# A token-mixing and LoRA feed-forward kernel: GpSimd's order of work ahead of the second pair of tiles

## The reference

```python
W = weights[condition]                                   # one 64x64 matrix of 16 for each batch
y = einsum('bct,bcd->bdt', x, W)
result = einsum('bnd,od->bno', y, W_base) + b_base
probs = softmax(einsum('bnd,ed->bne', y, W_gate))
top_p, top_i = top_k(probs, 2)                           # normalised to sum 1 -> route_w
h = einsum('bnd,erd->bner', y, A)
delta = einsum('bner,eor->bno', h * route_w[..., None], B)
out = x + result + delta * SCALING                       # SCALING = 1
```

## Time and profile before

| what | value |
|---|---|
| median of 3 runs | 952.94 us (952.38 to 955.5) |
| the profiled execution | 952.68 us, of which the span is 950.9 us |
| PE matmul busy | 938.5 us, 99% of the span |
| DVE, ACT, POOL busy | 430.8, 383.6, 543.9 us |
| chain that ended last | PE 93%, POOL 2%, each other engine or queue 1% or less |

### The profile page before, as it was taken

One profiled execution on the slowest core, in us unless ns is written; L12 is line 12 of the kernel. 1 busy time (PEld: TensorE's weight loads), 2 busy tenths in 40 slices (PEclk: granted clock), 3 DMA queues, 4 the chain that ended last, 5 costly groups with the idle time before them and its releaser, 6 DMA issues.

```text
span 950.9 us, 16849 instructions
## 1 busy us (share of the span) xinstructions
PE 938.5 (99%) x5462; PEld 881.5 (93%) x5462; DVE 430.8 (45%) x1333; ACT 383.6 (40%) x815; POOL 543.9 (57%) x514
## 2 busy tenths in 40 slices
PE   8899999999999999999999999999999999999998
PEld 6789999999999999999999999999999999999997
DVE  5774444434444434444444444344444344443444
ACT  6644434333344334343333343343433433433332
POOL 2956466545565554665555755556655557555560
PEclk9999999999999999999999999999999999999999
DMA  9333322233322333223333223332223332233312
GB/s 315 119 100 134 119 98 86 105 121 132 110 85 97 109 128 126 95 87 101 121 132 110 95 92 109 122 132 88 91 96 121 132 110 98 90 110 121 132 46 87
DMA packets 41452, 107.13 MB, mean 113 GB/s; under 512 B 4449, under 2 KB 8674, under 8 KB 41442
## 3 DMA queue, kind: packets, MB, share of 16 engines
q1 hardware_dynamic: 41440, 107.01, 32.7%
q10 hardware_dynamic: 2, 0.00, 0.0%
HBM read 73.43 MB, written 33.55 MB: 113 GB/s over the span
## 4 chain that ended last, share of the span: by engine, by line
PE 93%; POOL 2%; DMA 1%; issue 1%; SPq 1%; ACT 1%; DVE 1%; POOLq 0%; DVEq 0%
PE ps L791 55%; PE ps_r L791 18%; PE ps_out L809 10%; PE ps_out L819 9%; DMA w_sum<-in_w_t 1%; PE ps_hwt L815 1%; POOL s_lo L312 1%; POOL a_lo L308 0%; POOL s_sum L333 0%; ACT w_hi L416 0%; POOL s_sum L319 0%; SPq L220 0%; POOL s_sum L325 0%; SPq L224 0%; SPq L230 0%
## 5 line engine op out<-in xcount | busy, mean ns | idle before, releaser
L308 POOL TENSOR_TENSOR a_lo<-raw,a_hi 128x512 fp32r<-128x512 f32 x128 | 164.7, 1307 | 239.5 <-ACT a_hi L400 239.5
L610 DVE TENSOR_TENSOR z_sum<-ps,z_sum 128x448 f32<-128x448 f32 x155 | 96.8, 625 | 242.1 <-PE ps L791 242.0
L791 PE MATMUL ps<-w_hi,s_hi 128*128 128x448 f32 x496 | 183.7, 370 | 0.4 <-DVE z_sum L610 0.4
L791 PE MATMUL ps<-w_lo,s_hi 128*128 128x448 f32 x496 | 181.2, 365 | 0.0
L791 PE MATMUL ps<-w_hi,s_lo 128*128 128x448 f32 x496 | 179.7, 362 | 0.0
L791 PE MATMUL ps<-w_hi,a_hi 128*128 128x448 f32 x372 | 138.9, 373 | 3.4 <-POOL a_lo L308 3.4
L791 PE MATMUL ps_r<-r_lo,a_hi 128*128 128x264 f32 x496 | 140.8, 284 | 0.0
L791 PE MATMUL ps_r<-r_hi,a_hi 128*128 128x264 f32 x496 | 140.7, 284 | 0.0
L791 PE MATMUL ps_r<-r_hi,a_lo 128*128 128x264 f32 x496 | 140.6, 283 | 0.0
L791 PE MATMUL ps<-w_lo,a_hi 128*128 128x448 f32 x372 | 135.7, 365 | 0.0
L791 PE MATMUL ps<-w_hi,a_lo 128*128 128x448 f32 x372 | 135.6, 364 | 0.0
(11 more groups left out here) (97 smaller groups left out, 1592.9 us busy)
## 6 DMA issues: line engine op xcount, KB each, us to landing
raw<-in_x_t SPq DMA_DIRECT2D x128, 256.0 KB, 2.9
o_sb<-in_x SPq DMA_DIRECT2D x64, 512.0 KB, 3.9
out_x<-o_sb SPq DMA_DIRECT2D x62, 512.0 KB, 2.6
w_sum<-in_w_t SPq DMA_DIRECT2D x8, 448.0 KB, 9.3
r_raw<-in_w_t SPq DMA_DIRECT2D x4, 264.0 KB, 4.3
table_raw<-in_cond_w SPq DMA_DIRECT2D x2, 256.0 KB, 9.1
b_raw<-in_b_t SPq DMA_DIRECT2D x1, 512.0 KB, 11.0
out_x<-o_sb SPq DMA_DIRECT2D x2, 224.0 KB, 2.1
```

What stands on the lines that cost most here:

```text
L308: pool.tensor_tensor(a_lo[j][:], raw[j][:], as_f32(a_hi[j][:]), ALU.subtract).then_inc(s_a_lo[j], 1)
L610: return dve.tensor_tensor(to, bank[:, 0:NS], other, ALU.add)
L791: mm = pe.matmul(bank[:, 0:w.shape[-1]], a[:, k, :], w[:, k, :], start=(opens and k == 0 and q == 0), stop=(closes and k == KH - 1 and q = ...
```

## The change

POOL's order ahead of the second pair is written anew. The three sums S3, S1 and S2 stay first. Then the rests of A11 and A12 and the sum S4 come ahead of the rests of S3 and S1. No instruction is added or taken away, and nothing else in the program is touched.

```diff
             sum_s3(1, True)
             sum_s1(1, True)
             sum_s2(1, True)
-            s_rest(1, 3, s3[:], s3_hi, s3_lo)
-            s_rest(1, 1, s1[:], s1_hi, s1_lo)
             a_rest(1, A11)
             a_rest(1, A12)
             sum_s4(1)
+            s_rest(1, 3, s3[:], s3_hi, s3_lo)
+            s_rest(1, 1, s1[:], s1_hi, s1_lo)
             s_rest(1, 2, s2[:], s2_hi, s2_lo)
```

## The result

| | before | changed |
|---|---|---|
| median of 20 runs | 953.0 us (951.36 to 955.5) | 955.57 us (954.16 to 956.59) |
| the profiled execution | 952.68 us, span 950.9 | 955.73 us, span 954.0 |

The ratio is 1.0024, 95% interval 1.0018 to 1.0031: 0.24% slower, clear of noise but inside the 0.3% that the prediction counts as no change. The medians are 2.6 us apart, against 1.8 forecast; the prediction's limit for no change was 955.8, so 0.2 us were left.

The account below looks back on a forecast made before the run. PE, fully busy in the 29.00 us loop, was taken as the bound. P7 1.9 us later, less 0.1 at the LoRA wait, added 1.8 to the profiled 952.68: 954.5 us, range 951.0 to 956.8.

Parts of the forecast that it names:

- What bounds the kernel: In the loop PE is busy 29.00 of 29.00 us, so time won or lost before it stays so.
- What the change gives to PE: Second pair's start: P1 follows without idle at about 37.05, P2 starts at 40.50 instead of 45.66, 5.16 us earlier.
- What the earlier PE sets off: DVE's T rests shift 5.15 us onto POOL's A21, A22 and mix0 copies; taking turns, they delay PE's mixing to 54.73.
- The tie: DVE's rest of T3 against POOL's second copy into mix0: DVE starts 0.07 us before and goes first.
- The second case: Rival: the second copy into mix0 beats DVE's rest of T3; 951.2 to 952.8, centre 952.4 us; chance 0.28.
- The sum: From mixing at 54.73, 5.83 us of matmuls plus 1.67 for the clock: P7 at 62.2, 1.9 us later.
- The clock's fall: Behind PE's long idle ahead of the mixing, the lower clock costs 1.67 us, between 0 and 3.3.
- The wait at the LoRA rest: PE's later wait of 0.51 us for the LoRA rest at 69.90 may shrink; 0.1 us taken.
- No hindrance: Rival: POOL and DVE don't hinder each other, mix0 ready at 49.26, P7 5.2 us earlier; 947.5 us; chance 0.13.
- The slower case: Rival: DVE first, clock low twice as long behind PE's idle, another 1.67 us; 956.2 us; chance 0.14.

Follow-up runs that it names:

- experiment 2: Changed kernel with DVE's rest of T3 made to wait until both copies into mix0 are done: 952.69 us, ratio 0.9999.
- t1_holds: Changed kernel with DVE's rest of T1, and so that of T3, made to wait until mix0 is fetched: 951.08 us, ratio 0.9977.
- experiment 6: Changed kernel with POOL's rest of A12 and sum S4 moved behind the rests of S3 and S1: 950.4 us, ratio 0.9969.
- experiment 1: Changed kernel with the second pair's two copies into mix0 made ahead of the rest of S2: 949.85 us, ratio 0.9962.
- Experiment 8: Changed kernel with SP's load into A11 for the third pair held until the rest of S3 is made: 954.45 us, ratio 1.0023.
- filler: Changed kernel with 28 matmuls on zeros put in PE's gap ahead of the late mixing: 954.24 us, ratio 1.0011.
- filler_more: Changed kernel with 33 matmuls on zeros put in PE's gap ahead of the late mixing: 953.42 us, ratio 1.0008.
- 7: Kernel before, in its old order, with the two copies into mix0 made ahead of the rest of S2: 953.11 us, ratio 1.0002.
- 9: Changed kernel with early copies into mix0 and POOL's rests of A21 and A22 held until DVE's rest of T3: 955.09 us, ratio 1.0028.

## Why the prediction was right

**What bounds the kernel.** Right: the loop kept its full 29.00 us, and what PE lost ahead of it came out at the end, but for 0.4 us. ACT's copy of P1 comes 3.56 us later than before at the first loop pair (80.28 and 76.72) and 3.18 us at the last (921.10 and 917.92); no row shows where these 0.38 us went.

**What the change gives to PE.** Right. P1 starts without idle, P2 at 41.03 (40.50 and the 0.5 of the slow start), the last R matmul at 47.86 (47.22 and 0.64).

**What the earlier PE sets off.** Right in each step: T2's rest 2.72 us, A21 and A22 4.31, T1's rest 2.21, both copies above 2 us. Experiments 2 and 3 undo the meetings one by one by holding DVE, and the copies become short; experiment 6 does it by a later A12; 1 moves the copies out. Experiment 8 shows the same gap without the earlier load. That the earlier P2 is what moves DVE onto POOL is shown by 6 together with the profile.

**The tie.** Right, and steadier than its 0.07 us promised: DVE's T3 was first in the four profiled executions that leave the tie open (the changed kernel, `filler`, `filler_more`, `sp_later`), its second copy taking 2.11 us in each. The second case, at 0.28, was given too much; its time was right when experiment 2 forced it.

**The sum.** The gap is 7.25 us where 7.2 follow from the forecast's times. The clock's fall was mis-sized for this execution. From the mixing to P7 PE took 64.00 - 55.38 = 8.62 us, 2.79 above the 5.83 at full clock; the forecast took 1.67. The profiles in which PE waits for nothing else between the two give this, in us:

| kernel | gap ahead of the mixing | from the mixing to P7 | above 5.83 |
|---|---|---|---|
| changed | 7.25 | 8.62 | 2.79 |
| `sp_later` | 7.24 | 7.34 | 1.51 |
| `t3_holds` | 5.43 | 7.65 | 1.82 |
| `t1_holds` | 3.66 | 7.47 | 1.64 |
| `a12_later` | 2.18 | 5.94 | 0.11 |
| `filler` | 1.21 | 5.90 | 0.07 |

So 1.67 is near what three of the four long gaps cost, and the changed kernel's own profiled execution is the one far above it. A single price was wrong, and the two ends, 0 and 3.3, held all of them. P7's 3.69 us are about the forecast's 1.9, plus 0.65 for the later resumption (0.5 of it the slow start), plus 1.12 for the clock. The wait at the LoRA rest shrank by 0.08 us, from 0.51 to 0.43; 0.1 was taken. That the final number is as near as it is, 2.6 against 1.8, is in part luck: without the slow start P7 is 3.2 us late where 1.9 was forecast, and part of the difference is the 0.38 us of the loop, which nothing in the forecast foresaw.

**The rivals.** No hindrance (0.13) is refuted by the profile; its sign was right for what follows when the copies are out of the way (experiment 1). The slower case (0.14) named the clock as what could add to the forecast. It did, by two thirds of what that case gave, and its sign, a low stretch longer than 5 us, is there in this execution (0.50 over 5.9 us). In `sp_later`'s it is not: the clock is back at 1.00 from 58.50 us on, 3.1 us behind the gap.

## What to carry to other kernels

An engine that is late can shield its neighbours from each other. Before moving work ahead, shift everything that hangs on it by the gain, and look at what it lands on, here DVE instructions with two SBUF operands on POOL's. Then move the small thing that the critical engine waits for next, such as the 0.6 us of copies into `mix0`, ahead of the collision: the reorder alone lost 2.6 us, and with the copies moved it won 3.3. And before holding an engine back, see which load or buffer hangs on the end of its queue.

## What the runs showed of the hardware

The price of a PE gap in clock is not set by its length alone. A 7.25 us gap was followed by a clock of 0.50 over 5.9 us in one execution, and a 7.24 us gap by 0.74 over the same stretch in another. In `t1_holds` a gap of 3.66 us was followed by a clock of 0.50 from 53 to 55 us. In the profiled execution of `a12_later` the clock stayed at 1.0 behind gaps of 1.35 and 2.18 us, but four of that kernel's six executions have a mean of 0.998, so in most of them it did fall. The same shows in the kernel before: of the 29 executions beside the second group of experiments (7, 8, 9 and `filler_more`), three have a mean clock of 1.0 and took 950.49 to 951.51 us, nine have 0.996 and took 953.47 to 954.8. So much of the spread between executions of one kernel goes with the clock, though only the profiled ones show at which gap it fell. When DVE and POOL compete, a start 0.06 us earlier decided over 2 us, with the same winner, DVE, in each of four executions.
